# Mamba scan: the gate product y*silu(z) on GpSimd in place of VectorE

## What is computed

```python
def step(h, inp):
    u_t, dt_t, B_t, C_t = inp
    dA = jnp.exp(dt_t[:, :, None] * A)
    dBu = dt_t[:, :, None] * B_t[:, None, :] * u_t[:, :, None]
    h = dA * h + dBu
    y_t = jnp.einsum('bdn,bn->bd', h, C_t)
    return (h, y_t)
...
y = jnp.swapaxes(y, 0, 1) + D_param * x
y = y * jax.nn.silu(z)
return y @ out_proj_w
```

## Time and profile before

| | |
|---|---|
| median of 3 runs | 2629.27 us (2626.41 to 2630.71) |
| profiled execution | 2626.9 us |
| its span | 2625.2 us |
| busy in the span: PE, VectorE, ScalarE, GpSimd | 2275.7, 1809.7, 1324.6, 1331.5 us |
| first to last state product | 237.7 to 982.8 us |

### The profile page before, as it was taken

The page is one execution under the profiler, slowest core; times in us unless marked ns, Lnnn a source line. Parts: engine busy times, 40 slices in busy tenths (PEclk is TensorE's granted clock), DMA queues, the critical chain, the costliest instruction groups (busy, mean ns, idle before and its releaser), DMA issues. The chain is left out here.

```text
span 2625.2 us, 35522 instructions
## 1 busy us (share of the span) xinstructions
PE 2275.7 (87%) x11484; PEld 1341.2 (51%) x11485; DVE 1809.7 (69%) x2775; ACT 1324.6 (50%) x2531; POOL 1331.5 (51%) x996
## 2 busy tenths in 40 slices
PE   8995889989989985599975699999998549999998
PEld 3342445545545443499963334444445326666666
DVE  6998999999999995755545798889884651111200
ACT  5677887787788772122223546666665211111110
POOL 1545999898898990277755412222221012333332
PEclk9997999999999997699986789999999659999999
DMA  5458334133132104544446622212200322333322
GB/s 160 149 193 267 108 130 141 49 126 115 49 133 92 49 16 140 176 72 71 71 69 130 151 37 33 33 33 45 36 3 10 122 89 57 72 81 68 71 54 24
DMA packets 149684, 231.21 MB, mean 88 GB/s; under 512 B 26146, under 2 KB 98914, under 8 KB 149411
## 3 DMA queue, kind: packets, MB, share of 16 engines
q1 hardware_dynamic: 119202, 189.22, 23.5%
q0 software_dynamic: 30336, 40.16, 9.5%
HBM read 151.99 MB, written 81.66 MB: 89 GB/s over the span
## 5 line engine op out<-in xcount | busy, mean ns | idle before, releaser
L1163 POOL TENSOR_TENSOR scan_hC<-scan_h,scan_c_all 128x1024 f32<-128x1024 f32 x256 | 612.7, 2418 | 64.3 <-DVE scan_h L1083 63.2
L1083 DVE TENSOR_TENSOR_SCAN scan_h<-scan_dA,banks 128x1024 f32<-128x1024 f32 x224 | 504.5, 2275 | 21.0 <-ACT scan_dA L1038 12.9
L946 PE MATMUL banks<-scan_hC,all_ident 128*128 128x512 f32 x1024 | 484.8, 598 | 26.4 <-DVE scan_xc L1090 26.4
L2249 ACT ACTIVATE attn_pt<-banks 128x1024 f32<-128x1024 f32 (+3 forms) x384 | 292.2, 810 | 186.2 <-PE banks L2196 184.9
L1031 ACT ACTIVATE scan_scaled<-mamba_duT,mamba_bT 128x128 f32<-128x128 f32 x1024 | 312.1, 390 | 15.7 <-PE banks L923 15.5
L2133 POOL TENSOR_SCALAR_AFFINE_SELECT attn_pt<-attn_pt 128x256 f32<-128x256 f32 x256 | 104.1, 413 | 383.3 <-ACT attn_pt L2249 381.7
L2267 DVE TENSOR_REDUCE attn_m_lo<-banks 128x1 f32<-128x512 f32 (+3 forms) x432 | 266.9, 662 | 30.0 <-PE banks L2152 20.0
L946 PEld LDWEIGHTS banks<-scan_hC,all_ident 128*128 128x128 f32 x1024 | 184.9, 191 | 180.2 <-issue 129.6
L2923 DVE TENSOR_TENSOR ffn_y<-banks,ffn_gates 128x512 f32<-128x512 f32 x32 | 22.1, 692 | 358.5 <-PE banks L2822 351.8
L2759 POOL DMA_INDIRECT out<-ffn_y,ffn_ids x64 | 101.0, 1578 | 298.8 <-DVE ffn_y L2923 289.1
L2152 PE MATMUL banks<-attn_K,attn_Q 96*128 96x512 bf16 (+3 forms) x768 | 231.6, 340 | 12.0 <-DVE attn_mask L2261 11.0
(11 more groups left out here) (333 smaller groups left out, 3862.4 us busy)
## 6 DMA issues: line engine op xcount, KB each, us to landing
scan_c_all<-scratch_bc SPq DMA_DIRECT2D x64, 512.0 KB, 5.9
ffn_w<-in_e_w SPq DMA_DIRECT2D x16, 1024.0 KB, 5.3
attn_Q<-scratch_q SPq DMA_DIRECT2D x96, 128.0 KB, 3.9
scratch_x<-front_xc SPq DMA_DIRECT2D x8, 1024.0 KB, 5.2
scratch_z<-front_zs SPq DMA_DIRECT2D x8, 1024.0 KB, 7.3
scan_xc<-scratch_x SPq DMA_DIRECT2D x16, 512.0 KB, 3.5
scan_zs<-scratch_z SPq DMA_DIRECT2D x16, 512.0 KB, 4.5
scratch_dt<-front_lw SPq DMA_DIRECT2D x7, 1024.0 KB, 4.1
```

Of the source, the lines that this page charges most:

```text
L946: mm = pe.matmul(PS[:, YB + i, :], ident[:, :], hC[:, u % NHC, i * BANK:(i + 1) * BANK], start=s == 0, stop=s == NST - 1, skip_group_check ...
L1083: dve.tensor_tensor_scan(h[:, u % NH, :], decay, drive, 0.0, ALU.mult, ALU.add).then_inc(scanned, 1)
L1163: pool.tensor_tensor(hC[:, u % NHC, :], h[:, u % NH, :], c_all[:, s, :], ALU.mult).then_inc(hC_done, 1)
L2249: act.activation(pt[:, at % 4, 2 * pair:2 * pair + 2, 0:width], PS[:, ST + 2 * pair:ST + 2 * pair + 2, 0:width], ACT.Exp, scale=HD ** -0.5 ...
```

## The change

GpSimd computes the gate, with the same operands and the same result. In its program it stands at the head of slot 6 of the next group (FIN + 3), which is behind state product 5; for the chunk m = 0 it stands at the head of slot 14 (NST - 2), behind state product 13. VectorE keeps the D term and the last group's gate. GpSimd waits for the loads of xc and zs itself.

```diff
--- before.py
+++ after.py
@@ -1091,14 +1091,6 @@
                                          in1=PS[:, YB:YB + HALVES, :].rearrange("p a n -> p (a n)"),
                                          op0=ALU.mult, op1=ALU.add).then_inc(y_read, 1)
 
-            def gate_y(b, m):
-
-                G = b * MT + m
-                if m == 0 and not (isinstance(b, int) and b == 0):
-                    dve.wait_ge(out_added, TPB * b)
-                dve.wait_ge(y_read, G + 1)
-                dve.tensor_tensor(yz[:, m, :], xc[:, :], zs[:, :], ALU.mult).then_inc(yz_done, 1)
-
             def add_out(b, i):
                 k = b * TPB + i
                 dve.wait_ge(out_psum, k + 1)
@@ -1113,9 +1105,6 @@
                     step = out_step(m, s, out)
                     if step and step[1]:
                         add_out(b - 1, step[0])
-
-                    if s == (NST - 3 if before[1] == 0 else FIN) and not first:
-                        gate_y(*before)
                     if s < NST - 1:
                         times_b(b, m, s + 1)
                     elif not last:
@@ -1149,9 +1138,20 @@
                     pool.wait_ge(scanned, before + 1)
                 pool.tensor_tensor(dBu[:, :], du[m % 2][:, :], b_all[:, i, :], ALU.mult).then_inc(pool_bu, 1)
 
+            def gate_y(b, m):
+                G = b * MT + m
+                if m == 0 and b:
+                    pool.wait_ge(out_added, TPB * b)
+                pool.wait_ge(xz_in, 32 * (G + 1))
+                pool.wait_ge(y_read, G + 1)
+                pool.tensor_tensor(yz[:, m, :], xc[:, :], zs[:, :], ALU.mult).then_inc(yz_done, 1)
+
             def group(b, m, first, last, out):
+                before = (b, m - 1) if m else (b - 1, MT - 1)
                 for s in range(NST):
                     u = unit(b, m, s)
+                    if s == (NST - 2 if before[1] == 0 else FIN + 3) and not first:
+                        gate_y(*before)
                     for i, ps in enumerate(POOL_S):
                         if s == (POOL_S[i - 1] + 1 if i else 0):
                             drive(b, m, i, ps)
```

## The result

The changed kernel takes 2650.4 us (median of 4 runs, 2649.1 to 2651.6) against 2628.2 (2626.4 to 2630.7) of the kernel before beside it: the ratio is 1.0084, with a 95% interval of 1.0068 to 1.0100. The profiled execution has a span of 2649.6 us, 24.4 more than before. Forecast were 2655.3 and a range of 2641 to 2668.

The account below looks back on a forecast made before the run. VectorE was taken to set the pace in the scan stage, with room on GpSimd. Projection delay 24.0, clock 9.6 and gains -7.6 summed to +26.0 us: 2652.9 profiled, 2655.3 as median, range 2641 to 2668.

Parts of the forecast that it names:

- PE's later start at line 958: Groups m=0 of batches 1 to 3: PE starts the projection 8.0 us later, waiting for GpSimd's gate; 24.0 us.
- lower granted clock behind the gap: Behind PE's 8.9 us standstill in three m=0 groups the clock falls to 1.2 GHz, 3.2 us each; 9.6 us.
- the twelve other intervals: Groups m=1, m=2 and m=3 without VectorE's gate: 1.9 us gained per batch, -7.6 us in four batches.
- VectorE's stall before the first addition: Sign to look for: VectorE idle some 10 us before the first addition of lines 1103-1105 or scan 7, 3 times.
- The step that was mis-sized: Clock cost in m=0: 3.17 us of PE's time, seen after a 7.52 us gap elsewhere, taken as 3.2 us each.
- PE's longest gap in the scan: Before the change, PE's gaps in the scan are short, the longest 2.7 us, behind the D term.
- The step that failed: Group m=1: removing the gate behind scan 13 gains 0.93 us, not 1.62, since scan 15 waits for ScalarE; counted in every batch.
- That the clock stays up: Rival: same PE wait, but granted clock stays at 1.00 behind it; +16.4 us, 2645.7; chance 0.12.
- That the move would pay because the wait is covered: Rival: PE's wait for the gate in m=0 does not bind; only gains remain, -9.4 us, 2619.9; chance 0.08.
- That the gap costs more: Rival: slow stretch costs 6 us more PE time (+8.4) or moved product takes 3.26 us (+10.2); about 2664; chance 0.13.
- That VectorE would be slowed beside GpSimd's gate: Sign that the forecast is wrong: VectorE's scans grow longer beside GpSimd's gate; no size given.
- the first rival: Same PE wait in m=0, but granted clock stays at 1.00 behind it; +16.4 us, 2645.7; chance 0.12.

Follow-up runs that it names:

- e4: Changed kernel with 18 matmuls added on PE just ahead of its wait for the gate in the three m=0 groups: 2645.8 us, 1.0068 to the kernel before.
- e1: Changed kernel with GpSimd's gate of chunk 3 two slots earlier, at the head of slot 4: 2625.3 us, 0.9991 to the kernel before.
- e2: Changed kernel with the output projection begun three slots later on PE and the gate of chunk 0 in slot 15: 2622.0 us, 0.9981 to the kernel before.
- e3: Changed kernel with the gate of chunk 3 back on VectorE behind scan 3, 12 of 15 gates on GpSimd: 2622.9 us, 0.9983 to the kernel before.
- e7: Kernel before with only the gate of chunk 3 moved to GpSimd, at the head of slot 6 of the m=0 groups: 2658.2 us, 1.0119.
- e8: Kernel before with VectorE's gates of chunks 1 to 3 cut to one column, nothing given to GpSimd: 2618.5 us, 0.9967.
- e9: Kernel before with only the gates of chunks 1 and 2 on GpSimd, at slot 10, and SP's last-chunk load behind the tenth C row: 2621.5 us, 0.9973.
- e10: Kernel before with only the gates of chunks 1 and 2 on GpSimd, at slot 6, and SP's last-chunk load behind the sixth C row: 2623.5 us, 0.9981.

## Why the prediction was right, point by point

| term of the sum | forecast | measured |
|---|---|---|
| PE's later start at line 958, three groups | +24.0 | +23.1 |
| lower granted clock behind the gap | +9.6 | +4.9 |
| the twelve other intervals | -7.6 | -4.6 |
| in all | +26.0 | +23.4 in the stage |

**The wait.** Counted from the D term, PE began the projection 7.26 us behind it before (424.75 to 432.01) and 15.16 now (420.79 to 435.95): 7.9 us, and 7.3 and 7.9 in the other batches, where I had laid out 8.0 each from five GpSimd instructions of 2.33 us. Batch 2 is lower because PE had come there 0.6 us late before. The rows of the kernel before that this uses and the earlier trace rows does not show:

```profile
424.75 1.25 DVE L1090 SCALAR_TENSOR_TENSOR scan_xc<-scan_xc,mamba_d_par,banks 128x1024 f32<-128x1024 f32 x1
...
434.60 1.04 PE L923 MATMUL banks<-all_ident,scan_scaled 128*128 128x128 f32 x8
```

That nothing is made up behind it held as well: e4 leaves the wait alone, and 8.05 us of it stand in the interval. VectorE's stall before the first addition was forecast at 10 us and is 9.7 to 10.0. e1, e2 and e3 take all or nearly all of the wait away in three ways, and each is at or below the time of the kernel before.

**The clock.** The mechanism was right, the size wrong by half. The windows behind the first gate (us, PE busy, granted clock) show 0.57 and, from 440 on, full clock again:

```profile
435.00:440.00 5.00, 4.04 (x8) 0.57 0.57 206
440.00:445.00 5.00, 5.00 (x22) 1.00 0.02 5
```

From line 958's start to the transposes PE took 4.35, 4.20 and 4.14 us, and 2.59 before (432.01 to 434.60): 4.9 us in all. The step that was mis-sized is taking the 3.17 us from a gap of 7.52 in another stage. There the slow work lasted over three kinds of pieces, here for line 958's two matmuls and part of the next two of line 946 (2.64 us, not the double of 1.88 that was forecast). e4 gives 4.2 to 4.5 us for the same term. The term is no constant: in e7, behind the same gaps of 8.4 us, it is 7.1 us. The gap itself was laid out at 8.9 us and is 7.15 to 8.4. And the 2.7 us given as PE's longest gap in the scan is that of its weight loads; PE's own there is 1.9, and behind it the clock fell in at least one group (m=0 of batch 2) even before the change.

**The gains of the other groups.** In m=1 and m=2 of batch 0, scans, gates and the wait:

```profile
308.66 2.27 DVE L1083 TENSOR_TENSOR_SCAN scan_h<-banks,scan_dBu 128x1024 f32<-128x1024 f32 x1
...
317.21 2.29 DVE L1083 TENSOR_TENSOR_SCAN scan_h<-scan_dA,banks 128x1024 f32<-128x1024 f32 x1 [0.61 <-ACT scan_dA L1038]
...
339.11 2.35 POOL L1163 TENSOR_TENSOR scan_hC<-scan_h,scan_c_all 128x1024 f32<-128x1024 f32 x1
341.43 2.37 POOL L1147 TENSOR_TENSOR scan_yz<-scan_xc,scan_zs 128x1024 f32<-128x1024 f32 x1
...
343.75 9.30 POOL L1163 TENSOR_TENSOR scan_hC<-scan_h,scan_c_all 128x1024 f32<-128x1024 f32 x4
...
346.23 2.29 DVE L1083 TENSOR_TENSOR_SCAN scan_h<-scan_dA,banks 128x1024 f32<-128x1024 f32 x1 [0.65 <-POOL scan_hC L1163]
```

Scan 15 came 8.55 us behind scan 12, exactly as laid out from m=2. Product 6 of m=2 ends at 343.75 + 2.33 = 346.1, 37.4 behind scan 12 of m=1; laid out were 37.6 (310.93 to 348.5). Scan 9 waits 0.65 us for it, forecast 0.5 to 0.7; eight such waits make 5.2 us. The interval m=1 of batch 0 gains 1.25, where 0.93 was laid out. The interval m=2 gains 0.38 of VectorE's 1.07, m=3 0.38 as well where I had 0.6. The step that failed is m=1 in batches 1 to 3, where I carried the 0.93 us of batch 0 over to groups that also carry the projection. The kernel before, m=1 of batch 1, scan 12, the gate, and then scans 14 and 15:

```profile
500.64 2.28 DVE L1083 TENSOR_TENSOR_SCAN scan_h<-banks,scan_dBu 128x1024 f32<-128x1024 f32 x1
...
505.02 1.43 DVE L1100 TENSOR_TENSOR scan_yz<-scan_xc,scan_zs 128x1024 f32<-128x1024 f32 x1
507.68 4.46 DVE L1083 TENSOR_TENSOR_SCAN scan_h<-scan_dA,banks 128x1024 f32<-128x1024 f32 x2
```

and the changed kernel:

```profile
506.36 2.28 DVE L1083 TENSOR_TENSOR_SCAN scan_h<-banks,scan_dBu 128x1024 f32<-128x1024 f32 x1
...
512.48 2.29 DVE L1083 TENSOR_TENSOR_SCAN scan_h<-scan_dA,banks 128x1024 f32<-128x1024 f32 x1 [0.54 <-ACT scan_dA L1038]
...
515.45 2.29 DVE L1083 TENSOR_TENSOR_SCAN scan_h<-scan_dA,banks 128x1024 f32<-128x1024 f32 x1 [0.68 <-ACT scan_dA L1038]
```

Before, scan 15 started at 507.68 + 2.19 = 509.87, 9.23 behind scan 12. Now scan 14 waits for its decay too, 0.54, and scan 15 is at 9.09. Here ScalarE's chain is longer than in batch 0 (9.09 and not 8.55) and swallows the gate's 1.35 us (505.02 to 506.37) but for 0.1. That is 0.8 us in each of three groups, most of the 3.0 that the gains fell short.

**The rivals.** That the clock stays up is refuted by the window at 0.57. That the move would pay because the wait is covered is refuted by PE's 8.4 us; with the wait gone the gains left over are small, 4.9 us in the stage of e3, less than the 7.6 forecast. That the gap costs more is refuted as well: the slow stretch cost less than laid out, and the moved product took 2.36 us, not 3.26. That VectorE would be slowed beside GpSimd's gate: its scans take 2.277 us and took 2.275. By the rule of the Trainium skill (GPSIMD Engine Reference, Key points) only the VectorE gate with its two SBUF inputs contended, and the trace agrees: the slowest state product was 3.36 us before and is 2.40 now.

**Luck in the sum.** The clock's term was 4.7 us too high, the gains of the other groups 3.0 us too high, and the two errors partly cancel. The measured 2650.4 is about as near to the first rival's 2645.7 as to the forecast's 2655.3, so the time alone does not choose between them; the window at 0.57 and e4 do.

## What to carry to other kernels

An engine with idle time in its totals is not free at the moment a result is wanted: before moving an instruction, find the consumer that will stand in order behind it, and count the instructions of the new engine up to it. Here five instructions of 2.33 us in front of one wait cost more than VectorE's fifteen gates were worth. And price what is removed group by group: where PE or ScalarE sets the pace (m=0, and m=1 from batch 1 on), VectorE's gate was worth nothing to 0.1 us, elsewhere its full 1.07, and that only with the moved product put where its engine has caught up.

## What was not expected of the hardware

The granted clock of TensorE fell not only behind the 8 us gap. It fell in single groups behind a gap of 1.86 us (line 946 at 3.22 us in e8 and 3.65 in the changed kernel's batch 1, where 1.88 or 1.98 is usual), and in the same place of another batch or kernel it stayed up. Where it fell in the kernel before, e8, e9 and e10, the interval is 0.57 or 0.58 us longer (49.90 or 49.89, and 49.32). Shorter falls in e1 (batch 2, line 946 at 2.55 us) and e2 (batch 3, 2.59) left their intervals as they were. What decides between the two is open; I have not tried it.
